# Last convolution on sixteen 32x32 tiles of TensorE, with the image added by an identity matmul

## The reference, cut to what matters

```
x = x + L0(groupnorm(x))          # a row LSTM: 32 sequential steps, one image row each
x = x + L1(groupnorm(x))          # the last stage

groupnorm: 32 groups of 4 channels, eps 1e-5
L1: 3x3 convolution, padding 1, weights W (128, 128, 3, 3), then + sum(b, axis=1)
    mask: where (i - n) % 4 == 0 all nine taps of W[n, i] are kept, elsewhere only the centre tap
```

## Time and profile before

| | |
|---|---|
| runs | 649.73, 649.83, 656.97 us; median 649.83 |
| the profiled execution | 652.95 us, of which the span of instructions is 651.1 us |
| PE busy | 599.2 us (92%), 4968 matmuls and 4968 weight loads |
| DVE, ACT, POOL busy | 510.0 (78%), 470.3 (72%), 391.8 us (60%) |
| DMA | 89.29 MB, of which 16.78 MB written to memory; 46.7% of 16 engines by SP's queue, 10.0% by ACT's |
| mean granted clock of PE | 0.971 of full speed |

### The profile page before, as it was taken

One profiled execution on the slowest core, in us unless ns is written; L12 is line 12 of the kernel. 1 busy time (PEld: TensorE's weight loads), 2 busy tenths in 40 slices (PEclk: granted clock), 3 DMA queues, 4 the chain that ended last, 5 costly groups with the idle time before them and its releaser, 6 DMA issues.

```text
span 651.1 us, 14360 instructions
## 1 busy us (share of the span) xinstructions
PE 599.2 (92%) x4968; PEld 379.9 (58%) x4968; DVE 510.0 (78%) x1204; ACT 470.3 (72%) x838; POOL 391.8 (60%) x385
## 2 busy tenths in 40 slices
PE   1899899899999999999999999954999999999996
PEld 0344344578888888888888888842333333333332
DVE  5789875389999999999999999997577667677442
ACT  2579878699999999999999999965333433443320
POOL 2379848345555555555555555568667667777761
PEclk9799979899999999999999999995999999999999
DMA  9989920004432344442244443007798998989987
GB/s 232 271 236 268 217 35 0 10 4 65 66 54 35 45 66 65 66 66 41 31 61 65 66 65 57 11 1 190 206 276 253 269 282 248 288 265 270 261 273 204
DMA packets 96423, 89.29 MB, mean 137 GB/s; under 512 B 78240, under 2 KB 79520, under 8 KB 96288
## 3 DMA queue, kind: packets, MB, share of 16 engines
q1 hardware_dynamic: 89152, 69.47, 46.7%
q10 hardware_dynamic: 7200, 18.90, 10.0%
HBM read 35.07 MB, written 16.78 MB: 80 GB/s over the span
## 4 chain that ended last, share of the span: by engine, by line
PE 67%; SPq 13%; DVE 8%; DMA 6%; ACT 3%; issue 2%; POOL 1%; ACTq 1%; DVEq 0%; POOLq 0%
PE ps L1165 18%; PE ps L1143 12%; PE ps L1219 9%; PE ps L1170 9%; SPq L416 8%; PE ps L1147 6%; SPq L422 5%; DMA shifted<-pad 5%; PE ps L1088 5%; PE ps L1089 5%; PE ps L1209 2%; DVE bn L477 2%; DMA ident<-in_consts_dram 1%; ACT xn L899 1%; DVE img L744 1%
## 5 line engine op out<-in xcount | busy, mean ns | idle before, releaser
L823 POOL TENSOR_TENSOR fc<-gate,cell 128x352 f32<-128x352 f32 (+16 forms) x96 | 83.9, 874 | 144.6 <-ACT gate L973 144.6
L854 POOL COPY shifted<-pad 32x1073 f32<-32x1073 f32 x128 | 137.5, 1074 | 54.7 <-DVE pad L737 48.3
L1165 PE MATMUL ps<-z_hi,wg_hi 128*128 128x352 f32 (+13 forms) x384 | 134.2, 351 | 3.1 <-ACT z_hi L957 3.1
L1165 PE MATMUL ps<-z_hi,wg_lo 128*128 128x352 f32 (+13 forms) x384 | 122.4, 320 | 0.0
L1219 PE MATMUL ps<-shifted,wt_hi 128*32 128x512 f16 x1536 | 108.8, 390 | 9.0 <-DMA shifted<-pad 9.0
L1170 PE MATMUL ps<-z_lo,wg_hi 128*128 128x352 f32 (+13 forms) x384 | 107.5, 321 | 0.0
L973 ACT ACTIVATE gate<-ps,gate_bias 128x352 f32<-128x352 f32 (+16 forms) x192 | 104.2, 543 | 1.7 <-PE ps L1170 1.7
L744 DVE SCALAR_TENSOR_TENSOR img<-ps,y_unscale,img 128x512 f32<-128x512 f32 x64 | 47.8, 747 | 71.2 <-PE ps L1219 71.2
L973 ACT ACTIVATE ps<-ps,gate_bias 128x352 f32<-128x352 f32 (+16 forms) x192 | 99.5, 518 | 0.2 <-PE ps L1170 0.2
L1008 ACT ACTIVATE pad<-img,nbias,rstd 128x1024 f16<-128x1024 f32 x32 | 39.9, 1245 | 80.5 <-PE ps L1219 76.1
L833 POOL TENSOR_TENSOR img<-hT,xr 128x352 f32<-128x352 f32 (+1 forms) x96 | 88.8, 925 | 1.7 <-DVE hT L699 1.7
(11 more groups left out here) (121 smaller groups left out, 1116.5 us busy)
## 6 DMA issues: line engine op xcount, KB each, us to landing
shifted<-pad SPq DMA_DIRECT2D x128, 134.1 KB, 4.0
shifted<-pad ACTq DMA_DIRECT2D x128, 134.1 KB, 4.1
xr<-in_x_dram SPq DMA_DIRECT2D x64, 256.0 KB, 5.5
img<-in_x_dram SPq DMA_DIRECT2D x126, 128.0 KB, 3.6
out_dram<-img SPq DMA_DIRECT2D x60, 256.0 KB, 4.3
shifted<-shifted SPq DMA_DIRECT2D x2, 553.5 KB, 6.0
raw_c<-in_L_conv_W_dram SPq DMA_DIRECT2D x4, 144.0 KB, 2.7
out_dram<-img SPq DMA_DIRECT2D x8, 64.0 KB, 1.9
```

Source lines behind the costliest of these rows:

```text
L823: pool.tensor_tensor(fc[it % 2][:, 0:c1 - c0], gate[it % 2][0][:, 0:c1 - c0], cell[:, c0:c1], ALU.mult).then_inc(fc_done, 1)
L854: pool.tensor_copy(shifted[b % SLOTS][32:64, q, ROWS_AT:ROWS_END].bitcast(F32), pad[b % SLOTS][32 * q:32 * q + 32, ROWS_AT:ROWS_END].bitca ...
L1165: pe.matmul(gbank(it, m)[:, 0:n], w[:, GATE_ORDER[m], :], z_hi[it % 2][:, 0:n], start=(w is wg_hi), stop=False)
```

## The change

The last stage works on groups of two images (`PAIR` = 2, 16 groups) instead of half images. The 2048 pixels of a pair are cut into four pieces c of 512 pixels. A PSUM bank no longer holds all classes of one half image; it holds one output class q of all four pieces, piece c on partitions 32c to 32c+31. So the output of input rows 32q and piece c comes from the array's tile at row 32q, column 32c, and the sixteen tiles are all used.

- `dense(g)`: for each class q, three terms by four matmuls (128 rows by 32 columns, one for each piece).
- `residual(g)`: sixteen float32 matmuls of 32x32 tiles with a scaled identity `ident_y`, which put the image itself into the bank.
- `tiled(g)`: three terms by eight taps by sixteen matmuls of 32x32 tiles, read from `pad` in place (`window`), each with its own weight load.
- `finish_class(g, q)`: the bank times a scale plus a bias, written over the pair's part of `img`; classes 0 and 2 by ACT, 1 and 3 by DVE. Scales and biases for each class come from one small matmul in the preparation.
- `store_group(g)`: four DMAs from SP for each pair, which sort the classes back.
- All copies to `shifted`, the rearranged weights, the ones, and POOL's part in the stage are gone. `xn` moves from PSUM to on-chip memory, two of them; `pad` has four slots; PE rotates over seven banks. DVE takes the upper statistics of eight images in the LSTM's last eight items (`HELD` = 8) instead of four.

The diff, cut to its core:

```diff
+HELD = 2 * CH
-SLOTS = 3
+SLOTS = 4
+PAIR = 2
+GROUPS = B // PAIR
+PIECE = PAIR * HW // Q
+PIECE_ROWS = PIECE // W
+Y_BANKS = 7
+TERMS = (("hi", 0), ("lo", 0), ("hi", 1))
+TAPS = [(d, e) for d in range(3) for e in range(3) if (d, e) != (1, 1)]
+ACT_CLASSES, DVE_CLASSES = (0, 2), (1, 3)
...
+        def window(b, part, row, d, e):
+            at = LOW_AT * part + ROWS_AT + (row + d - 1) * PADW + e - 1
+            return pad[b % SLOTS][:, at:at + PIECE_ROWS * PADW].rearrange("p (h w) -> p h w", w=PADW)[:, :, 0:W]
+
+        def piece(g, c):
+            return PAIR * g + c * PAIR // Q, c * PIECE_ROWS % H
+
+        def y_bank(g, q):
+            return ps[:, (Q * g + q) % Y_BANKS, :]
+
+        def group_out(g, q):
+            return img32[:, PAIR * g:PAIR * g + PAIR].rearrange("p b h w -> p (b h w)")[:, PIECE * q:PIECE * (q + 1)]
...
+        def store_group(engine, g, pieces):
+            for c in pieces:
+                r = slice(32 * c, 32 * c + 32)
+                b, row = piece(g, c)
+                engine.dma_start(out_q[:, :, b, W * row:W * row + PIECE].rearrange("q n x -> n q x"),
+                                 img32[r, PAIR * g:PAIR * g + PAIR].rearrange("p b h w -> p (b h w)")
+                                 .rearrange("p (q x) -> p q x", q=Q)).then_inc(stored, 16)
...  SyncE
-            for b in range(B):
-                shift(b)
-                if b % 2 and b > 2:
-                    store_pair(b - 3)
-            store_last(sp, QUARTERS[:2])
+            for g in range(GROUPS):
+                sp.wait_ge(out_act, len(ACT_CLASSES) * (g + 1))
+                sp.wait_ge(out_dve, len(DVE_CLASSES) * (g + 1))
+                store_group(sp, g, range(Q))
...  VectorE
-                if ITEMS - CH <= it < ITEMS:
+                if ITEMS - HELD <= it < ITEMS:
...
+            def finish_class(g, q):
+                v.wait_ge(conv_done, g + 1)
+                v.tensor_scalar(group_out(g, q), y_bank(g, q), finish[:, 1, q:q + 1], finish[:, 0, q:q + 1], ALU.mult,
+                                ALU.add).then_inc(out_dve, 1)
...
+            for g in range(GROUPS):
+                k = (g + 3) // 2
+                chain = g % 2 == 1 and k < CHUNKS
+                near, far = PAIR * (g + 2), PAIR * (g + 5)
+                finish_class(g, DVE_CLASSES[0])
+                if chain:
+                    chain_mean(FIRST_CHUNKS + k)
+                finish_class(g, DVE_CLASSES[1])
+                if far < B:
+                    image_stats_again(far)
+                if chain:
+                    chain_var(FIRST_CHUNKS + k)
+                if near < B:
+                    lo(near)
+                if chain:
+                    chain_rstd(FIRST_CHUNKS + k, k % 2)
+                if far < B:
+                    image_stats_again(far + 1)
+                    if g % 2 == 0:
+                        bn_aggr(FIRST_CHUNKS + (g + 4) // 2)
+                if near < B:
+                    lo(near + 1)
...  ScalarE
             def high(b):
                 if b >= SLOTS:
-                    act.wait_ge(pads_used, b - SLOTS + 1)
+                    act.wait_ge(conv_done, (b - SLOTS) // PAIR + 1)
...
+            for g in range(GROUPS):
+                k = (g + 3) // 2
+                near = PAIR * (g + 2)
+                for q in ACT_CLASSES:
+                    finish_class(g, q)
+                if near < B:
+                    if near % CH == 0:
+                        act.wait_ge(gn_step, GN_STEPS * (FIRST_CHUNKS + near // CH + 1))
+                    high(near)
+                    norm(near)
+                if g % 2 == 1 and k < CHUNKS:
+                    square_root(FIRST_CHUNKS + k)
+                if near < B:
+                    high(near + 1)
+                    norm(near + 1)
...  TensorE
+            def dense(g, terms, first):
+                for q in range(Q):
+                    if first:
+                        bank_free(g, q)
+                    for m, (w, part) in enumerate(terms):
+                        for c in range(Q):
+                            b, row = piece(g, c)
+                            pe.matmul(rows(out_rows(g, q, c)), WALL[w][:, 1, 1, 32 * q:32 * q + 32],
+                                      window(b, part, row, 1, 1), start=first and m == 0, stop=False,
+                                      tile_position=(0, 32 * c), skip_group_check=True)
+
+            def residual(g):
+                for q in range(Q):
+                    for c in range(Q):
+                        b, row = piece(g, c)
+                        r = slice(32 * q, 32 * q + 32)
+                        pe.matmul(out_rows(g, q, c), ident_y[r, r],
+                                  img32[r, b, row:row + PIECE_ROWS].rearrange("p h w -> p (h w)"), start=False, stop=False,
+                                  tile_position=(32 * q, 32 * c), skip_group_check=True)
+
+            def tiled(g, terms, last):
+                for m, (w, part) in enumerate(terms):
+                    for d, e in TAPS:
+                        for q in range(Q):
+                            for c in range(Q):
+                                b, row = piece(g, c)
+                                r = slice(32 * q, 32 * q + 32)
+                                ins = pe.matmul(rows(out_rows(g, q, c)), WALL[w][r, d, e, r], window(b, part, row, d, e)[r],
+                                                start=False, stop=last and m == len(terms) - 1 and (d, e) == TAPS[-1],
+                                                tile_position=(32 * q, 32 * c), skip_group_check=True)
+                if last:
+                    ins.then_inc(conv_done, 1)
...
+            pe.wait_ge(hi_done, PAIR)
+            dense(0, TERMS[:2], True)
+            sum_means(FIRST_CHUNKS + 1)
+            residual(0)
+            tiled(0, TERMS[:2], False)
+            pe.wait_ge(lo_done, PAIR)
+            sum_vars(FIRST_CHUNKS + 1)
+            dense(0, TERMS[2:], False)
+            tiled(0, TERMS[2:], True)
+            for g in range(1, GROUPS):
+                k = g // 2 + 1
+                chain = g % 2 == 0 and k < CHUNKS
+                if chain:
+                    sum_means(FIRST_CHUNKS + k)
+                pe.wait_ge(lo_done, PAIR * (g + 1))
+                dense(g, TERMS, True)
+                if chain:
+                    sum_vars(FIRST_CHUNKS + k)
+                residual(g)
+                tiled(g, TERMS, True)
```

More of the change, by code:

```diff
@@ L736, in lo @@
                 v.wait_ge(hi_done, b + 1)
-                v.tensor_tensor(interior(pad[b % SLOTS], 1), xn.rearrange("p (h w) -> p h w", w=W),
+                v.tensor_tensor(interior(pad[b % SLOTS], 1), rows(xn[b % PAIR][:]),
                                 interior(pad[b % SLOTS], 0), ALU.subtract).then_inc(lo_done, 1)
-            def residual(b):
-                for s in range(2):
-                    half = image(b)[:, HW // 2 * s:HW // 2 * (s + 1)]
-                    v.wait_ge(conv_done, 2 * b + s + 1)
-                    v.scalar_tensor_tensor(out=half, in0=y_bank(b, s), scalar=y_unscale[:], in1=half,
-                                           op0=ALU.mult, op1=ALU.add).then_inc(sum_done, 1)
+            def finish_class(g, q):
+                v.wait_ge(conv_done, g + 1)
+                v.tensor_scalar(group_out(g, q), y_bank(g, q), finish[:, 1, q:q + 1], finish[:, 0, q:q + 1], ALU.mult,
+                                ALU.add).then_inc(out_dve, 1)
             v.wait_ge(row_done, ROW_AHEAD + ITEMS - 2)
@@ L837, in _ @@
             forget(0)
+            pool.memset(pad[1][:].bitcast(F32), 0.0).then_inc(pads_zero, 1)
             for it in range(ITEMS + 1):
@@ L1018, in norm @@
             def norm(b):
[L1019 to L1032 removed]
+                if b >= PAIR:
+                    act.wait_ge(lo_done, b - PAIR + 1)
@@ L1035, in _, with finish_class @@
+                whiten(rows(xn[b % PAIR][:]), b, b // CH % 2, b % CH).then_inc(xn_done, 1)
+            def finish_class(g, q):
+                act.wait_ge(conv_done, g + 1)
+                act.activation(group_out(g, q), y_bank(g, q), ACT.Identity, bias=finish[:, 0, q:q + 1],
+                               scale=finish[:, 1, q:q + 1]).then_inc(out_act, 1)
             act.activation(warm[:, 3:4], warm[:, 0:1], ACT.Sqrt).then_inc(warmed, 1)
             square_root(FIRST_CHUNKS)
-            for b in range(B):
-                if b % CH == 0:
-                    act.wait_ge(gn_step, GN_STEPS * (FIRST_CHUNKS + b // CH + 1))
-                high(b)
-                norm(b)
-                if b:
-                    shift(b - 1)
-                if b % CH == 2 and b < B - CH:
-                    square_root(FIRST_CHUNKS + b // CH + 1)
@@ L1047, in _ @@
-            shift(B - 1)
-            store_last(act, QUARTERS[2:])
+            act.wait_ge(gn_step, GN_STEPS * (FIRST_CHUNKS + 1))
+            act.wait_ge(row_done, ROW_AHEAD + ITEMS)
+            high(0)
+            high(1)
+            norm(0)
+            norm(1)
```

(23 more changed lines are left out.)

276 lines of the change are left out of this document (74 added, 202 removed).

## The result

The changed kernel takes 697.66 us (median of 4 runs, 695.46 to 700.26), the kernel before, run beside it, 650.78 (4 runs, 649.73 to 656.97): a ratio of 1.070, 95% interval 1.062 to 1.078. It is slower by 7%, where 6% faster was forecast.

A forecast was written before the change was run, and what follows sets the result against it. The prediction took PE's own rounds in the last stage as the bound. A group fell from 11.8 to 9.8 us; 15 such groups after group 0, plus the end, gave span 612.6 and median 611 us, range 592 to 672.

The forecast's parts named there:

- the price of a round of sixteen: Outer taps in `tiled`: 0.24 us for each of 24 rounds of sixteen tiles, 5.76 us a group.
- supply makes it slower: Rival, PE's queue in `tiled`: instruction packets fetched one at a time; 672 us at 0.40 a round, 738 at 0.57; chance 0.10.
- Row tiles take turns: Rival, outer taps: four row groups share the array's time, 28.2 us a group, near 905 us; chance 0.12.
- The identity: Float32 matmuls of `residual`, taken as four passes, 0.89 us a group; two rounds (0.45) to sixteen (3.6) possible.
- The changes of tiling: PE's two changes between full array and column tiles, 0.11 us each, 0.22 a group.
- The statistics: Two small matmuls on PE, 0.24 us each in every second pair before; 0.24 a group in the sum.
- The group's sum: PE's work per group in the last stage: 2.67 + 5.76 + 0.89 + 0.22 + 0.24 = 9.8 us against 11.8.
- The start: PE starts the last stage with the high part at 447.1 us, including 2.0 us of LSTM delay.
- ACT and DVE set no pace: Rival "ACT and DVE set the pace": a group takes their chain instead of PE's, 10.6 us, 623 us; chance 0.12.
- Starts of different tiles: PE: loads to different tiles start some 6 ns apart; the skill's 25 ns rule would give 0.40 us a round, near 672.
- The end: After the last matmul: hand-off 0.2, two finishes 1.3, store issues and last landing 3.1; 6.7 us in all.
- The clock: PE's clock starts low, 1.2 GHz, rises some 3.3 us after unbroken work begins; full after the first 4 us.

The follow-up runs named there:

- e6: Changed kernel, all tap rounds but the last as four 128x32 tiles instead of sixteen 32x32, other classes' taps left out there; 614.27 us.
- b1: Kernel before with its dense matmul issued as four column tiles of 128x32, so PE never changes tiling; ratio 1.000.
- e2: Changed kernel with only the first row group's four tiles in each tap round but the last, other classes' taps left out; 648.76 us.
- e1: Changed kernel with each outer-tap matmul streaming 256 columns instead of 512; 705.97 us, ratio 1.081.
- b3: Kernel before with each tap matmul cut into four of 128 columns, same columns, four times the instructions; 786.04 us.
- e7: Changed kernel without the low-weights outer taps; from group 1 on identity first, then per class three dense and four tap rounds; 635.10 us, ratio 0.973.
- e4: Changed kernel, complete, from group 1 on each third of the dense rounds ahead of its third of the taps; 694.99 us, ratio 1.062.
- e8: Changed kernel, complete, from group 1 on identity first, then per class three dense and six tap rounds; 692.42 us, ratio 1.062.

## Why the prediction was wrong

**The step that failed** is the price of a round of sixteen: "I take 0.24, between 0.2225 and 0.26, as these are maxima". A group took 15.0 us and not 9.8; over 24 rounds the 5.2 us above the sum are 0.22 a round, 0.46 in all where the prediction called 0.36 the bound above. The bound came from the earlier trace rows: sixteen instructions within 0.18 us. That row is true, and the bursts agree with it (256 in 1.74 us, 6.8 ns each). But it lies inside one block of instructions, and the prediction stretched it over 768. A rate seen over sixteen instructions bounds nothing that refills every 256; over long stretches the price is 3.45 us a block at least, 13.5 ns an instruction, and 16 in the mean.

**The rival that came true** is "supply makes it slower": one packet of 16 KB under way at a time, its full trip counted. Its break-even, 0.34 us a round, and its time for 0.40, 672 us, are consistent with what came: at 0.46 it gives 611 + 16 x 24 x 0.22 = 695. It stood at 0.10. It had the mechanism too: 7.6 rounds a packet and a trip of 1.9 to 4.3 us, where eight rounds a packet and 3.45 us at the least were found. The packet count of the earlier trace rows had led to 242 instructions a packet, against 256 found. What spoke for more than 0.10 was in the earlier trace rows: 542 matmuls and loads in 20 us, 9.4 us for 256, and nowhere in that run do 256 of PE's take less than 7.6. A trip of 3.5 us could not show there, so the absence of stops was no evidence against it; I read it as cover.

The Trainium skill (Advanced Engine Details and Errata, "ISA Cache") states that an engine's instruction cache has lines of 16 KB, 256 instructions, and only two of them; for TensorE it gives 128 KB all the same, which would be eight such lines. The traces agree on the 256 and on the 16-KB packets, and with one block in use and one on its way; how many lines there are no run here shows by itself. What a refill costs the page doesn't state; here it is 3.45 us at the least (1.10 to the packet, 2.35 to the next instruction).

**What held.** By e6 and the trace after:
- Sixteen tiles run together: 0.22 us a round inside a burst. "Row tiles take turns" (0.12) is out.
- The dense part: rounds 0.22 us apart. The identity, taken as four passes or 0.89 us: 555.24 to 556.12, 0.88. The changes of tiling, 0.22 a half: b1. The statistics, 0.24 a group, cost 0.31 in e6 (its last groups, which have none, take 9.46).
- The group's sum, 9.8: e6's 9.77, and 9.5 in the changed kernel without its stops (below). The whole span without the failed term, 612.6: e6's 612.5. The agreement is closer than the terms are: the round was taken 0.02 us too long, which e6 makes up by two more changes of tile shape.
- The start: 447.1 forecast, 447.81 measured, from whitening that begins 2.9 us later than in the earlier trace rows.
- ACT and DVE set no pace: in e6 a group every 9.77 us left both idle for over a third of the time (73.6 and 79.6 of 124 us busy). My 0.65 us for a finish was short (0.77 on ACT, 0.81 on DVE), with no effect.
- Starts of different tiles: in the burst 128 matmuls start in 1.74 us, 13.6 ns apart. The Trainium skill (TensorE: Matmul & The Clock Gate, "Wait — 56ns, not 53.3ns?") has them never closer than about 25 ns; across tiles the trace doesn't agree. The 672 us that the prediction worked out by that rule were nearer the result than its own 611, for another reason.

**Small misses.** The end took 8.4 us after the last matmul and not 6.7. The timeline of the end:

```profile
688.18 1.45 ACT L952 ACTIVATE img<-ps,finish 128x512 f32<-128x512 f32 x2 [14.80 <-PE ps L1181]
688.18 1.53 DVE L683 TENSOR_SCALAR img<-ps,finish 128x512 f32<-128x512 f32 x2 [14.72 <-PE ps L1181]
689.78 3.21 SPq L340 DMA_DIRECT2D out_dram<-img  x4
```

The stores wait for both finishes (1.6 us) and take 3.21 us to issue, and the last lands 3.5 us later. The clock was forecast at full after group 0; it is 0.94 from 476 to 600 us, in a stage in which PE is idle for 29 of these 124 us. It is no second cause of weight: in the group from 552.45 to 567.12 it is 1.00, and the group still takes 14.67 us, against 15.0 in the mean. The three stops there add up to 5.2 us (from the last start before a stop to the first after it), and the rest is 9.5, inside the sum's 9.8.

The account of the span: 696.5 - 612.6 = 83.9 us, of which 0.7 is the start, 1.7 the end, and 81.5 the groups (240.3 against 158.8).

## What to carry to other kernels

Before a large matmul is cut into small tiles, count instructions as well as columns: a tile round that keeps the columns and multiplies the instructions is free only while 256 instructions of PE last longer than a refill, here 3.5 to 4.4 us, 14 to 17 ns each. A rate from a short burst says nothing about a stream; look for the longest stretch that ran at the rate you want to assume, and where there is none, carry the bound at the packets you can see. And of two bounds that lie together, as PE and the copies here, taking one away shows only the other: ask what the new arrangement's own floor is before counting the gain.

## What was not expected of the hardware

- PE's clock fell from 1.00 to 0.50 while PE was busy without a break, after taps that used one of four row groups (e2); with the same counts on all 128 rows it stayed at 1.00 (e6). The profile's busy time doesn't tell the clock; the granted clock has to be read beside it. e1 ran at 0.75 with half the columns.
- A fetch of the next block starts 1.1 us after a stopped PE goes on (1.7 in b3, beside the shift copies), but about 2 us after an entry without a stop in the changed kernel and e7 (1.1 in e4). Spreading slow work evenly gained 5 us (e8) and not the 13 to 38 that I expected. The cause stays open.
- The mean price of a block lies between 3.96 and 4.43 us in all eight kernels that stop, but single blocks differ. In the changed kernel a block of taps alone costs 3.45 us at its cheapest and 4.0 to 4.8 where it is entered without a stop; one with a group's whole dense part and identity takes 4.7 to 5.3 us of work (6.7 at a clock of 0.66) and ends without a stop.
